# A Mamba layer with its feed-forward part: causal blocks by quarters, and TensorE's tile loop in pairs throughout

## What is computed

```python
proj = einsum('bsd,ed->bse', x, in_proj_w)           # gate, hs, B, C, dt
hBC = silu(conv4(hBC) + conv_b)                      # causal over tokens
L = exp(_segsum(A_dt))                               # 0 where s > l
Y_diag = einsum('bzlhn,bzshn,bhzls,bzshp->bzlhp', Cc, Bc, L, xch)
states = einsum('bzlhn,bhzl,bzlhp->bzhpn', Bc, decay_states, xch)
Y_off = einsum('bzlhn,bzhpn,bhzl->bzlhp', Cc, prev, exp(A_cum))
Y = Y_diag + Y_off + hs * D
g = Y * silu(gate);  out = rmsnorm_per_group(g) * norm_w @ out_proj_w.T
```

## Time and profile before

| | |
|---|---|
| median of three runs | 1747.42 us |
| the profiled run, on the device | 1747.38 us |
| its span | 1745.3 us |
| TensorE matmul busy | 1712.1 us (98%) |
| VectorE busy | 1263.2 us (72%) |
| GpSimd busy | 1194.7 us (68%) |
| ScalarE busy | 846.3 us (48%) |
| one group, as all of them | steps of 15.1 us, the third of 15.7; seventh and eighth step and window together 89.4 us |

### The profile page before, as it was taken

How to read it: one execution, slowest core, us unless ns; L and a number is a source line. 1 busy time by engine, 2 the same in 40 slices (tenths; PEclk the granted TensorE clock), 3 DMA queues, 4 the chain that set the end, 5 groups by cost and what they waited for, 6 DMA issues and landing times.

```text
span 1745.3 us, 34624 instructions
## 1 busy us (share of the span) xinstructions
PE 1712.1 (98%) x10520; PEld 1403.5 (80%) x10520; DVE 1263.2 (72%) x1894; ACT 846.3 (48%) x1275; POOL 1194.7 (68%) x868
## 2 busy tenths in 40 slices
PE   6999999999999999999999999999999999899998
PEld 5788888888888888888888888888888787688887
DVE  6888648863887288728883788468845887877777
ACT  4666346643664366435653665356634663222221
POOL 3599559964897489757985799569955988423330
PEclk9999999999999999999999999999999999999999
DMA  3333012211231123102220222023201211111101
GB/s 102 99 90 85 23 50 91 86 30 43 79 92 43 31 80 92 55 19 85 80 73 19 73 80 85 19 61 85 86 12 56 92 56 64 49 37 49 48 13 48
DMA packets 71341, 107.23 MB, mean 61 GB/s; under 512 B 16740, under 2 KB 25060, under 8 KB 71304
## 3 DMA queue, kind: packets, MB, share of 16 engines
q1 hardware_dynamic: 70296, 105.38, 20.4%
q10 hardware_dynamic: 1008, 1.38, 0.3%
HBM read 103.51 MB, written 3.15 MB: 61 GB/s over the span
## 4 chain that ended last, share of the span: by engine, by line
PE 84%; DVE 9%; issue 4%; ACT 1%; DVEq 1%; DMA 0%; POOL 0%; ACTq 0%
PE proj L839 15%; PE proj L841 14%; PE proj L840 14%; PE y L999 8%; PE y L969 6%; PE y L971 6%; PE y L970 6%; DVE v L1168 3%; PE y L983 3%; PE y L839 1%; PE y L841 1%; PE y L840 1%; DVE hs L1182 1%; PE decay L943 1%; PE decay L839 1%
## 5 line engine op out<-in xcount | busy, mean ns | idle before, releaser
L839 PE MATMUL proj<-xhi,w_hi 128*128 128x512 f32 x1072 | 432.8, 404 | 3.8 <-DVE gate L1187 3.6
L841 PE MATMUL proj<-xhi,w_lo 128*128 128x512 f32 x1072 | 419.5, 391 | 0.0
L840 PE MATMUL proj<-xlo,w_hi 128*128 128x512 f32 x1072 | 419.5, 391 | 0.0
L1168 DVE SCALAR_TENSOR_TENSOR v<-proj,par_sb,v 128x510 f32<-128x510 f32 x378 | 275.2, 742 | 20.8 <-DVE v L1168 9.7
L477 POOL TENSOR_TENSOR g_lo<-gated,g_hi 128x512 fp32r<-128x512 f32 x127 | 163.0, 1286 | 183.6 <-ACT g_hi L716 183.5
L839 PEld LDWEIGHTS proj<-xhi,w_hi 128*128 128x128 f32 x1072 | 201.8, 188 | 63.4 <-issue 14.4
L495 POOL TENSOR_TENSOR gated<-hs,gate 128x512 f32 (+1 forms) x126 | 188.5, 1517 | 71.9 <-DVE hs L1299 71.9
L841 PEld LDWEIGHTS proj<-xhi,w_lo 128*128 128x128 f32 x1072 | 201.8, 188 | 43.2
L840 PEld LDWEIGHTS proj<-xlo,w_hi 128*128 128x128 f32 x1072 | 202.2, 189 | 37.8
L438 POOL TENSOR_TENSOR w_lo<-w_raw,w_hi 128x512 fp32r<-128x512 f32 x144 | 182.0, 1283 | 55.0 <-ACT w_hi L593 55.0
L612 ACT ACTIVATE v<-proj,par_sb 128x512 f32<-128x512 f32 x126 | 98.1, 779 | 238.9 <-PE proj L841 238.9
(11 more groups left out here) (198 smaller groups left out, 3336.8 us busy)
## 6 DMA issues: line engine op xcount, KB each, us to landing
w_raw<-in_win SPq DMA_DIRECT2D x144, 256.0 KB, 2.7
fade_l<-faded SPq DMA_DIRECT2D x128, 256.0 KB, 3.3
wo_raw<-in_wout SPq DMA_DIRECT2D x64, 256.0 KB, 2.7
M<-in_w SPq DMA_DIRECT2D x14, 512.0 KB, 3.8
row_r<-rows SPq DMA_DIRECT2D x256, 3.0 KB
row_l<-rows SPq DMA_DIRECT2D x256, 3.0 KB
cb<-in_w SPq DMA_DIRECT2D x7, 512.0 KB, 3.2
out<-resid SPq DMA_DIRECT2D x8, 256.0 KB, 2.0
```

The lines of the kernel that those rows point to most:

```text
L839: e.matmul(o, hi_l, hi_r, start=first, stop=False)
L840: e.matmul(o, hi_l, lo_r, start=False, stop=False)
L841: return e.matmul(o, lo_l, hi_r, start=False, stop=last)
L1168: e.scalar_tensor_tensor(dst[:, :, d:S], src[:, :, 0:S - d], weights(K - 1 - d), dst[:, :, d:S], ALU.mult, ALU.add)\
```

## The change

Half of the tokens are kept in reverse order inside each chunk, from the silu on: for tokens 512 to 1023 (batches 2 and 3) ScalarE's tanh and VectorE's silu read their source backwards, 128 tokens at a time, so that hs, gate, xdt, M and gated hold those chunks turned round; the heads' dt, C (its first tile; the others go through `hs_silu`), the mask and the running sums are made to match. The convolution itself still runs in natural order. Where tokens must come out in order again (the sum of squares, the upper and lower parts of g) the turned half is read backwards. In a turned chunk the zero quarter of the triangle is the opposite one.

`y` then leaves the zero quarter out. Per batch and head it makes the past product over 128 columns; the product over the 64 columns that need all 128 rows; and the product over the other 64 columns, which needs 64 rows. The last kind uses rows 0 to 63 in batches 0 and 1 and rows 64 to 127 in batches 2 and 3, and four of them stand next to each other: two row halves by two column halves of the array. 24 matmuls of a step become 40. Both banks' `yready` now come at the end.

On TensorE alone `over_tiles` becomes `over_pairs`: four pairs in the loop, none written out in groups 0 to 6. So the eighth step also makes exponents, for a ninth tile (the next group's first). Nobody reads these; the window makes them again. The semaphore `dready` counts two more per group. The other four engines keep `over_tiles`.

At the start GpSimd makes two more triangular constants and a bf16 copy of the masks.

```diff
+def over_pairs(eng, step, window):
+    with eng.Fori(0, G - 1) as g:
+        with eng.Fori(0, TPG // 2) as p:
+            step(g, 2 * p, 0, True, True, True)
+            step(g, 2 * p + 1, 1, True, True, True)
+        window(g, True)
+    with eng.Fori(0, TPG // 2 - 1) as p:
+        step(G - 1, 2 * p, 0, True, True, True)
+        step(G - 1, 2 * p + 1, 1, True, True, True)
+    step(G - 1, TPG - 2, 0, True, False, True)
+    step(G - 1, TPG - 1, 1, False, False, False)
+    window(G - 1, False)
...
-        after, bias_bc, nega_bc = [sq[:, i * P:(i + 1) * P] for i in range(3)]
+        after, bias_bc, nega_bc, after_back = [sq[:, i * P:(i + 1) * P] for i in range(4)]
+        sums = [hs[:, 1, i * P:(i + 1) * P] for i in range(2)]
-        upto = sb("upto", [P, P])
+        upto = sb("upto", [P, 2, P], BF16)
...
+        def turned_round(ap, h):
+            ap = ap.rearrange("p (c l) -> p c l", l=P)
+            return ap[:, :, ::-1] if h else ap
...
-        dready = Tally(sem("diff_ready"), 0, OWN)
+        dready = Tally(sem("diff_ready"), 0, OWN, OWN)
...
+        def tokens(t, kk):
+            ap = gated[:, 4 * kk:4 * kk + 4, t * P:(t + 1) * P]
+            return ap[:, :, ::-1] if t >= TT // 2 else ap
...
@@ GpSimd: constants, g_lo, sum of squares
+            e.affine_select(out=sums[1], in_=sums[1], compare_op=ALU.is_ge, fill=0.0,
+                            base=0, pattern=[[-1, P]], channel_multiplier=1).then_inc(s_sums, 1)
+            e.memset(after_back, 1.0).then_inc(s_sums, 1)
+            pool.wait_ge(s_sums, 2)
+            e.affine_select(out=after_back, in_=after_back, compare_op=ALU.is_gt, fill=0.0,
+                            base=0, pattern=[[1, P]], channel_multiplier=-1).then_inc(s_sums, 1)
+            pool.wait_ge(s_const, 6)
+            e.tensor_copy(upto[:, :, :], hs[:, 1, 0:2 * P].rearrange("p (z l) -> p z l", z=2)).then_inc(s_sums, 1)
...
-                e.tensor_tensor(g_lo[:, i % 2, :, :], gated[:, 4 * kk:4 * kk + 4, t * P:(t + 1) * P],
-                                g_hi[:, i % 2, :, :].bitcast(F32), ALU.subtract).then_inc(glo.sem, 1)
+                e.tensor_tensor(g_lo[:, i % 2, :, :], tokens(t, kk), g_hi[:, i % 2, :, :].bitcast(F32), ALU.subtract)\
+                    .then_inc(glo.sem, 1)
...
-                    e.tensor_tensor(halves(sqacc, h), halves(sqacc, h), square, ALU.add)\
+                    total = turned_round(halves(sqacc, h), 0)
+                    e.tensor_tensor(total, total, turned_round(square, h), ALU.add)\
                         .then_inc(sacc.sem, 1)
@@ ScalarE: dt heads, both tanh, g_hi (the same way)
-                e.activation(halves(dst, h), v[:, h, :], ACT.Tanh).then_inc(tanh.sem, 1)
+                e.activation(turned_round(halves(dst, h), 0), turned_round(v[:, h, :], h), ACT.Tanh)\
+                    .then_inc(tanh.sem, 1)
...
@@ TensorE
+            pe.wait_ge(s_sums, 3)
...
+                    def block(b, z, head, rows, part, inputs, slot, start, stop):
+                        first, width = part
+                        at = (b % 2) * S + z * P + first
+                        return e.matmul(ybank[b // 2][head * HD:(head + 1) * HD, at:at + width],
+                                        inputs[rows, head * HD:(head + 1) * HD],
+                                        M[rows, slot + head, b * P + first:b * P + first + width],
+                                        start=start, stop=stop)
+                    every, whole, low, high = slice(0, P), (0, P), (0, HD), (HD, HD)
                     for b in range(B):
-                        cols = slice(b * P, (b + 1) * P)
-
-                        for z, part, slot, inputs in ((0, 0, 0, xdt[:, 2 * b, :]), (1, 0, 4, xfade[:, b, :]),
-                                                      (1, 1, 2, xdt[:, 2 * b + 1, :])):
+                        for head in range(2):
+                            block(b, 1, head, every, whole, xfade[:, b, :], 4, not b % 2, False)
+                    for b in range(B):
+                        for z in range(2):
                             for head in range(2):
-                                mm = e.matmul(
-                                    ybank[b // 2][head * HD:(head + 1) * HD,
-                                                  (b % 2) * S + z * P:(b % 2) * S + (z + 1) * P],
-                                    inputs[:, head * HD:(head + 1) * HD], M[:, slot + head, cols],
-                                    start=(part == 0), stop=(part == z))
-                        if b % 2:
-                            mm.then_inc(yready.sem, 1)
+                                block(b, z, head, every, (high, low)[b // 2], xdt[:, 2 * b + z, :], 2 * z, False, False)
+                    for b in range(B // 2):
+                        for z in range(2):
+                            final = b == 1 and z == 1
+                            for other in range(2):
+                                for head in range(2):
+                                    mm = block(b + 2 * other, z, head, slice(other * HD, (other + 1) * HD),
+                                               (low, high)[other], xdt[:, 2 * (b + 2 * other) + z, :], 2 * z,
+                                               False, final)
+                                if final:
+                                    mm.then_inc(yready.sem, 1)
...
-            over_tiles(pe, step, window)
+            over_pairs(pe, step, window)
@@ VectorE (gate_silu and the first C tile the same way)
-                e.scalar_tensor_tensor(halves(dst, h), halves(dst, h), 1.0, v[:, h, :], ALU.add, ALU.mult)\
+                kept = turned_round(halves(dst, h), 0)
+                e.scalar_tensor_tensor(kept, kept, 1.0, turned_round(v[:, h, :], h), ALU.add, ALU.mult)\
                     .then_inc(silu.sem, 1)
...
+                dve.wait_ge(s_sums, 4)
-                mask = upto[:, :].unsqueeze(1).broadcast_to([P, B, P])
+                mask = upto[:, :, :].unsqueeze(2).broadcast_to([P, 2, 2, P])
```

More of the change, by code:

```diff
@@ L193, in mamba_ffn @@
         s_marks = sem("batch_marks_copied")
+        s_sums = sem("sums_made")
         s_wdt_split = sem("wdt_split")
@@ L395, in _ @@
             e.memset(ident[:, :], 0.0).then_inc(s_const, 1)
-            e.memset(upto[:, :], 1.0).then_inc(s_const, 1)
+            e.memset(hs[:, 1, 0:2 * P], 1.0).then_inc(s_const, 1)
             e.memset(after, 1.0).then_inc(s_const, 1)
@@ L401, in _ @@
                             base=0, pattern=[[-1, P]], channel_multiplier=1).then_inc(s_const, 1)
-            e.affine_select(out=upto[:, :], in_=upto[:, :], compare_op=ALU.is_ge, fill=0.0,
+            e.affine_select(out=sums[0], in_=sums[0], compare_op=ALU.is_ge, fill=0.0,
                             base=0, pattern=[[1, P]], channel_multiplier=-1).then_inc(s_const, 1)
@@ L602, in _ @@
                 act.wait_ge(s_dtp, h + 1)
-                e.copy(halves(dt_heads, h), ybank[h][:, :]).then_inc(s_dtc, 1)
+                e.copy(turned_round(halves(dt_heads, h), 0), turned_round(ybank[h][:, :], h)).then_inc(s_dtc, 1)
             def tap3(h, weights, nready, vfree, banks=proj):
@@ L622, in hs_tanh @@
                 act.wait_ge(taken.sem, ntaken)
-                e.activation(halves(dst, h), v[:, h, :], ACT.Tanh).then_inc(tanh.sem, 1)
+                e.activation(turned_round(halves(dst, h), 0), turned_round(v[:, h, :], h), ACT.Tanh)\
+                    .then_inc(tanh.sem, 1)
             def gate_tanh(dst, h, nready, banks=proj):
                 act.wait_ge(ready.sem, nready)
-                e.activation(halves(dst, h), banks[h][:, :], ACT.Tanh, scale=0.5).then_inc(tanh.sem, 1)
+                e.activation(turned_round(halves(dst, h), 0), turned_round(banks[h][:, :], h), ACT.Tanh, scale=0.5)\
+                    .then_inc(tanh.sem, 1)
             act.wait_ge(s_dtv, 2)
@@ L715, in g_upper @@
                 act.wait_ge(glo.sem, glo.window(g, i - 1))
-                e.copy(g_hi[:, i % 2, :, :], gated[:, 4 * kk:4 * kk + 4, t * P:(t + 1) * P]).then_inc(ghi.sem, 1)
+                e.copy(g_hi[:, i % 2, :, :], tokens(t, kk)).then_inc(ghi.sem, 1)
             def step(g, j, par_, nxt, nxt2, ahead):
@@ L904, in _ @@
             pe.wait_ge(s_dta, 1)
+            pe.wait_ge(s_sums, 3)
             for c in range(TT):
                 mm = e.matmul(ybank[c // 4][:, (c % 4) * P:(c % 4 + 1) * P], dta[:, c * P:(c + 1) * P],
-                              upto[:, :], start=True, stop=True)
+                              sums[c // 4], start=True, stop=True)
             mm.then_inc(s_cum, 1)
             for b in range(B):
-                mm = e.matmul(misc[:, b * P:(b + 1) * P], after, dta[:, 2 * b * P:(2 * b + 1) * P],
+                mm = e.matmul(misc[:, b * P:(b + 1) * P], after if b < B // 2 else after_back, dta[:, 2 * b * P:(2 * b + 1) * P],
                               start=True, stop=True)
@@ L1186, in gate_silu @@
                 dve.wait_ge(tanh.sem, ntanh)
```

(10 more changed lines are left out.)

## The result

The changed kernel takes 1731.87 us (median of four runs, 1730.87 to 1732.87) against 1747.51 (median of four runs of the kernel before; 1761.38 is one of them): 15.6 us or 0.9% less. The ratio of the runs side by side is 0.9871, with a 95% interval of 0.9828 to 0.9913; that of the medians is 0.9911. The kernel before has single longer runs, such as the 1761.38, and the changed kernel has none; the part on the length of the code comes back to them. The profiled run took 1731.54 us, its span is 1729.4.

A forecast was written before the change was run, and what follows sets the result against it. TensorE, 98% busy, was taken as the bound, with a second loop through GpSimd and VectorE close behind. Steps 14.5, window 1.9 and last group 0.2 sum to 16.6 us off 1747.38: 1730.7 us, range 1726 to 1756.

The forecast's parts named there:

- rival A: Whole kernel: the forecast itself, 1727 to 1736 us, as the window's and the queue's terms fall; chance 0.60.
- lost step: TensorE's step of 15.67 us instead of 15.11, when L484 overtakes L1182; claimed to go.
- TensorE's code: Code per group two steps shorter, each step longer; claimed no price in the trace of either.
- second loop: GpSimd to L1182 to L1299 to GpSimd: 14.97 us against TensorE's new 14.93; nothing waits within seven steps.
- The new `y`: TensorE's `y` in each step: 2.44 us, 0.18 less than 2.62, with 64-column slots at 0.058 us.
- change of shape: TensorE's array changing shape, once more per step, before the quarters: 0.10 us.
- register work: TensorE's work between `y` and `exponents`, partly exposed behind the short quarters: 0 to 0.1 us, taken as 0.07.
- Rival C: TensorE's `y`: matmul starts become the bound, `y` 2.85 us, 0.23 more than now; kernel 1762 us; chance 0.14.
- The steps: TensorE's steps become 14.93 us, seven turns 104.5; 1.8 us less per group, 14.5 us for eight groups.
- The ninth exponents: Step 7 on TensorE: they cost 0.30 us, covered by the 0.39 wait; window 0.27 us earlier, 1.9 in all.
- At no cost: Two `yready` at the end, backwards reading, bf16 mask and start constants: claimed free, the constants at most 0.4 us.
- Rival D: GpSimd's L516: backwards reading is slow; at twice its time 5.9 us per group more, 1794 us; chance 0.07.

The follow-up runs named there:

- r1: The changed kernel with TensorE back on the loop of before, so without the ninth tile's exponents; 1770.38 us, ratio to the kernel before 1.0117.
- r5: The changed kernel with 32 instead of 64 columns streamed in the 16 matmuls of 128 rows, leaving out half that product; 1731.96 us, one run.
- r7: The kernel before with the two squares of every tile moved from GpSimd to ScalarE; 1738.85 us, ratio 0.9948.
- r3: The changed kernel with whole 128 x 128 blocks in `y`, keeping the turned chunks and the new loop; 1747.67 us, ratio 0.9984.
- r6: The changed kernel with the two squares of every tile moved from GpSimd to ScalarE; 1729.07 us, ratio 0.9875.
- r10: The kernel before, old loop, with the first chunk's blocks in `y` as two 64-column halves, 32 matmuls; 1788.91 us, ratio 1.0213.
- r9: The kernel before, old loop, with the second chunk's blocks in `y` as two 64-column halves, 40 matmuls; 1790.91 us, ratio 1.0224.
- r4: The changed kernel with all quarter matmuls on rows 0 to 63 before those on rows 64 to 127; 1752.0 us, ratio 1.0000.

## Why the prediction was right, and where it was not

The time was forecast at 1730.7 us and is 1731.9, and the mechanism named, rival A, is there: four quarters in a slot, no lost step. Three steps of the prediction failed all the same. It put TensorE's code at no price and without a reason, and r1 shows a price of 23 us for the new `y` in the old loop. It had the second loop at 14.97 us, with no wait in seven steps, which by its own words makes it wrong; the loop takes 15.03 in the mean, and TensorE waits. And it took one per cent as the least that a measurement can tell, and so gave 0.56 to "within one per cent", where the whole interval, 0.9% to 1.7% faster, lies away from no change. That the point came within 1.2 us is in part luck: terms that were off by more than that cancel. By its steps:

*The new `y`.* Forecast 2.44 us and 2.60 from its first record to the exponents; measured 2.60. Past products 0.92 with the 0.05 of their start, pairs in slots of 0.058, quarters four at a time. Two small terms were off and cancel: the change of shape takes 0.14 us, not 0.10, and of the register work that was to show (0.07) only 0.02 does. r5 shows why 0.058 from the variances was the right row: the slot does not follow the columns streamed, so the weights are left. Rival C needed more than 0.015 us per start; four quarters start within each 0.058, so it falls, and with it a reading across quarters of the Trainium skill's floor of 25 ns between starts ("TensorE: Matmul & The Clock Gate", section "Wait — 56ns, not 53.3ns?").

*The steps.* No lost step, as said, and r7 shows the cause from the other side: take GpSimd's load away and the lost step goes without a shorter `y`, for 8.7 us. But the second loop isn't 14.97 us. In every second step GpSimd begins `gated` (L534) 0.43 us after L1364's first half instead of 0.34. r3 has the same 0.43 with whole blocks, so it comes with the turned chunks, though no instruction of GpSimd is longer; what holds it there stays open. By the ends of GpSimd's pair L477 the loop takes 14.97 to 15.00 and 15.05 to 15.10 us by turns, 15.03 in the mean, and uses up the slack sooner: from step 2 on TensorE waits a little. Seven turns take 104.77 instead of 104.5. Over the seven groups of the loop the steps bring 11.1 us by the starts of the turns, where 12.7 of the 14.5 were forecast for them. In r6, without that loop, the 104.5 are there.

*The price of a wait.* One more term was missing. Timeline of the changed kernel's step 4, TensorE's `unit(0)`:

```profile
495.95 0.39 PE L883 MATMUL proj<-xhi,w_lo 128*128 128x512 f32 x1
496.21 0.50 PE L881 MATMUL proj<-xhi,w_hi 128*128 128x512 f32 x1
496.55 0.39 PE L882 MATMUL proj<-xlo,w_hi 128*128 128x512 f32 x1
496.78 0.39 PE L883 MATMUL proj<-xhi,w_lo 128*128 128x512 f32 x1
```

L881 was due at 495.95 + 0.23 = 496.18 and came at 496.21, a wait of 0.03 us. But its successor starts 0.34 later instead of 0.23, and some of the next ones 0.24 later. The step is 15.10 instead of 14.93: 0.17 for a wait of 0.03. The same lies behind the earlier trace rows: between the two kernels the window's first matmul moved by 0.30 us against its turn, the second by 0.42, the ninth by 0.47.

*The ninth exponents.* Forecast: the window starts 0.27 us earlier. Measured, from the turn to the window's first matmul 12.20 us instead of 12.50, 0.30; and with the restart that is gone too, step 7 and window are 73.85 instead of 74.33, 0.48 less. In one group of the kernel before the lost time falls into step 6 instead (15.56 us, then 73.74), so that over the seven groups it is 2.6 us instead of 1.9. The last group brings 2.0, as forecast, and the first step begins 0.3 us earlier, which nobody forecast. So the steps' term was oversized by 1.6 us and this one undersized by 0.7: 11.1 + 2.6 + 2.0 + 0.3 = 16.0 where 16.6 were forecast (the spans differ by 15.9), and the medians have 15.6.

*At no cost.* Reading backwards: L556 takes 1288 ns in the mean where L516 took 1287, the tanh of hs 632 and `gate_silu` 674 in both kernels. Rival D falls; what is left of it is the 0.09 us in every second step.

*TensorE's code.* "I see no price in the trace of either" holds for the two together in the profiled runs. But as an argument it was empty: the trace of a code that fits cannot show what one costs that doesn't. The longer step alone costs 23 us (r1), the shorter round takes them away, and a rival in which the code's length decided was not among the five. Of the new `y` in the old loop, r1, I forecast 1729.8, and it was 1770.4. The price may even stand in the kernel before: 27 of its 63 runs are longer by 5 to 23 us and none of the 48 on the new loop is. If these are fetches, the change takes away a cost that the sum had at nothing, and that is why the ratio stands at 1.3% where sum and medians have 0.95% and 0.90%; this part is argued, not shown.

*The numbers.* Range and point hold. The chances put 0.56 on a change within 1% and 0.34 on more than 1% faster. The forecast stood at 0.95%, next to the bound. The runs of each kernel on the new loop lie within 3 us of each other, and the shorter runs of the kernel before within 4, so a gain of 16 us was not a thing "about what a measurement can tell": the doubt was whether rival A would come, and 0.60 for it should have gone further to the side of faster.

## What to carry to other kernels

Before a stage that is written out inside a loop is made longer, count the records of one round on that engine; if a jump back costs some microseconds under "issue" and the instruction queue shows a multiple of its packets, roll the loop up, even if that adds work. Price a wait of TensorE with its restart, about 0.15 us on top of its length. And when a fast engine is let run ahead, look for the place at which a second loop of nearly the same length overtakes: relieving its busiest member (r7) brought more than half of what the shorter product did.

## What the runs showed that I had not expected

- A round of TensorE's loop with 1549 records is not fetched again in the profiled run, one of 1677 is in each round: up to 4 or 5 us of silence (3.9 in r10, 4.1 in r9, 5.1 in r1), nine to ten packets of 16 KB, and 1.2 us more at the lower clock level; 6.3 us in r1's third group against the changed kernel.
- The kernel before has a tail of longer runs (27 of 63), which no kernel on the shorter round has (0 of 48).
- A matmul on rows 64 to 127 starts before earlier ones in the program on rows 0 to 63 (r4: 449.61 against 449.66 to 449.78). Starts on different row halves are not in program order.
- Four matmuls on the four quarters of the array start within one slot of 0.058 us (444.754 to 444.774 in the changed kernel).
- An f32 matmul with 64-column weights has slots of 0.058 us per pass whether 1, 32 or 64 columns are streamed.
- A negative step in an operand makes no instruction longer, on GpSimd (1288 ns against 1287), ScalarE (632 in both) or VectorE (674 in both).
